# First routed stage of a two-layer macaron transformer: plain indirect writes by first and second choice, added on VectorE, in place of indirect additions to DRAM

## The chip, the cores and the metric

One core of one Trainium2 chip runs the whole network in one program. The metric is the device time of one execution in microseconds, lower is better; the kernel before was timed in three runs. TensorE is the matrix engine (PE in the profile), VectorE is DVE, ScalarE is ACT, GpSimd is POOL and SyncE is SP, which issues most DMAs. The rows "POOLq" and "SPq" are the instruction queues that issue DMAs.

## The reference

Input: x, 8 sequences of 512 tokens of width 128, so 4096 tokens in 32 tiles of 128.

```
x = x + 0.5 * ffn0(layernorm(x))       # 8 experts of 256, top 2, no capacity
x = x + attn0(layernorm(x))            # 32 heads of 32
x = x + 0.5 * ffn0(layernorm(x))
x = x + 0.5 * ffn1(layernorm(x))       # first routed stage
x = x + attn1(layernorm(x))            # 16 heads of 64
x = x + 0.5 * ffn1(layernorm(x))       # second routed stage
```

ffn1 sends each token to its two best experts of eight. Each expert has room for 640 tokens and takes those with the largest weights; what exceeds the room is dropped, so a token may get results from two, one or no expert. An expert computes `(silu(x wg) * (x wu)) wd`, and its row is multiplied by the token's normalised weight and added to the token.

## The kernel before

**Order.** Every engine has an instruction stream of its own, and semaphores tie them. `program_order` gives each part of the work a hand-written start and end on a common scale (the table `WHEN`), sorts the calls, and each engine plays the same list with its own generators, one step per call. So where an engine's instruction stands in its queue is fixed by hand. The parts in order: feedforward 0 (`compute0`, `prepare0`) over 8 sequences and 8 experts; attention 0, 64 groups (8 sequences, 8 groups of heads); feedforward 0 again, with the router of layer 1 beside it (`route`, `keep`); the first routed stage (`experts1(0)`); attention 1, again 64 groups, with `ahead` preparing the next sequence and `route` its router; the second routed stage (`experts1(1)`).

**X** holds the residual of all 4096 tokens on chip. A sequence of 512 tokens is a batch in the code. `x_done[b]` is the event after which VectorE may use sequence b of it.

**The routed stage.** VectorE searches each expert's threshold (`search`), numbers the places (`positions`), and ends with `token_of`: for each of 8 x 5 x 128 slots the number of its token row. It comes from two small matmuls, over the number within a tile and the number of the tile (`tile_number`, written by ScalarE as 1 to 32 for both choices; the choices stand one after the other in it). Empty slots get one of 640 extra rows behind the 4096. Per expert, GpSimd issues five gathers (`gather_rows`, line 1970), each of 128 rows of 544 bytes from the DRAM tensor `tokens`; TensorE turns them (line 785), computes gate and up in three split products each (line 780), and the down projection (line 1115); ScalarE writes the weighted rows to `rows_out` (line 1409), and GpSimd issues five scatters of 128 rows of 512 bytes (`scatter_rows`, line 1982). A scatter is an indirect DMA with `compute_op=ALU.add`. GpSimd's queue is: gathers of experts 0, 1, 2, scatters of 0, gathers of 3, scatters of 1, and so on. Scatters of expert e wait for those of e - 1 to have landed, since two of them may add to the same row.

In the first routed stage the scatters add into the DRAM tensor `sums`. `keep` (SP, line 2084) has stored X there, sequence by sequence, during the second feedforward; at the end SP waits for the last scatter and loads X back with 8 DMAs of 256 KB (line 2003), and attention 1 begins with the layernorm of sequence 0 (line 1441 on VectorE, then GpSimd, then ScalarE, then TensorE's transposes). In the second routed stage the scatters add into the output.

**Attention 1.** For every group, TensorE computes q, k, v (line 780), the scores for the maxima and for the probabilities (line 902), the weighted sums (line 945) and the sums of probabilities (line 984). VectorE takes maxima (line 1583), reciprocals (line 1614), the mixed result (line 1627) and the low halves of q and k (line 1557), which free the banks that the scores of the next group need. GpSimd adds probability tiles (line 1947), two operands on chip. `normalise` (line 1447) is the first step of `ahead` for the next sequence: four statistics and four aggregations, between the reciprocals of a group.

```
def scatter_rows(e):
    pool.wait_ge(sums_stored, 16 * BATCHES * (s + 1))
    if s or e:
        pool.wait_ge(*(all_scattered(s, e - 1) if e else all_scattered(0, EXPERTS - 1)))
```

## Time and profile before

| what | value |
|---|---|
| median of three runs | 3053.96 us (3050.08 to 3054.35) |
| profiled execution | 3044.68 us, span of its trace 3042.9 us |
| busy, share of the span | PE 92%, DVE 69%, ACT 57%, POOL 57% |
| chain that ended last | PE 31%, DVE 4%, POOL 4%, the rest under 10% |
| DMA | 151 MB, mean 50 GB/s |

| stretch, us | what runs | PE busy | DVE busy | POOL busy |
|---|---|---|---|---|
| 0 to 228 | feedforward 0 | 210.65 | 143.83 | 15.55 |
| 228 to 1440 | attention 0 | 1186.84 | 870.50 | 993.02 |
| 1440 to 1640 | feedforward 0, router | 184.35 | 141.67 | 20.51 |
| 1640 to 1699 | first search and places | 16.47 | 45.21 | 0.00 |
| 1699 to 1849 | first routed stage | 107.88 | 53.04 | 106.64 |
| 1849 to 2840 | attention 1 | 960.63 | 756.00 | 509.13 |
| 2840 to 3042 | second search and routed stage | 122.55 | 93.41 | 104.32 |

The profiled execution is the one that every time in the text comes from; it was 9 us shorter than the median of the runs. A busy engine in such a table is not yet the bound: for each stretch one has to ask which wait ends last. In the trace's rows a bracket tells how long the engine was idle before the row and what it waited for; rows that follow each other without one had no wait worth showing.

### The profile page before, as it was taken

Reading aid. Unit: us, or ns where it says so; the run is one execution under the profiler, and the core shown is the slowest. Engines: PE = TensorE matmul, PEld = TensorE weight load, DVE = VectorE, ACT = ScalarE, POOL = GpSimd, SP = SyncE. Lnnn points to the kernel's source line nnn. Section 1 sums busy time; section 2 is a strip of 40 time slices with the busy share of each in tenths; the row PEclk is TensorE's granted clock in tenths of the full one; section 3 lists DMA queues with packets and bytes.
Section 4 is the critical chain, followed back from the end, with each engine's and each line's share of the span. In section 5 each row is a group of like instructions: output and inputs, shape, how many; then the busy total and the mean of one; then the engine's idle time right before and its main releaser. Section 6 shows DMA issues by size and latency. Waiting matters only on the chain. (4 is left out here: it accounts for less than half of the span.)

```text
span 3042.9 us, 49798 instructions
## 1 busy us (share of the span) xinstructions
PE 2789.4 (92%) x17716; PEld 1926.3 (63%) x17716; DVE 2103.6 (69%) x4494; ACT 1735.3 (57%) x3334; POOL 1749.2 (57%) x1540
## 2 busy tenths in 40 slices
PE   7999999999999999999995686999999999999376
PEld 6995555556555565647884584666666666665276
DVE  5667777777776777765776535877878778777642
ACT  5665767676776767676773334554545445445033
POOL 0004989898988888893100473555545555555067
PEclk9999999999999999999997798999999999999588
DMA  3004443343344344330002241000000000000033
GB/s 100 1 7 99 96 92 87 86 104 85 91 92 92 85 92 98 85 78 18 15 23 67 61 69 34 2 5 5 8 5 5 5 9 5 5 5 9 28 80 54
DMA packets 127654, 151.32 MB, mean 50 GB/s; under 512 B 29939, under 2 KB 69424, under 8 KB 126896
## 3 DMA queue, kind: packets, MB, share of 16 engines
q1 hardware_dynamic: 113328, 137.41, 18.5%
q0 software_dynamic: 14080, 10.73, 2.6%
q8 instruction: 143, 2.34, 0.3%
q14 instruction: 103, 0.84, 0.1%
HBM read 31.34 MB, written 14.57 MB: 15 GB/s over the span
## 5 line engine op out<-in xcount | busy, mean ns | idle before, releaser
L1947 POOL TENSOR_TENSOR arena<-arena 128x512 f32<-128x512 f32 x1152 | 1444.5, 1281 | 591.6 <-ACT arena L1304 557.3
L1583 DVE TENSOR_REDUCE top<-psum 128x1 f32<-128x512 f32 x1536 | 973.1, 678 | 193.4 <-PE psum L902 124.4
L1304 ACT ACTIVATE arena<-psum 128x512 f32<-128x512 f32 x1536 | 838.0, 599 | 237.9 <-PE psum L902 141.1
L894 PE MATMUL psum<-stack 96*128 96x512 f32 (+1 forms) x2048 | 648.2, 440 | 16.3 <-ACT arena L1304 9.1
L894 PEld LDWEIGHTS psum<-stack 96*128 96x128 f32 (+1 forms) x2048 | 345.9, 190 | 211.5 <-DVE top L1583 81.5
L945 PE MATMUL psum<-arena,values 128*32 128x512 f32 (+1 forms) x3072 | 476.6, 595 | 3.4 <-ACT arena L1304 3.4
L945 PEld LDWEIGHTS psum<-arena,values 128*32 128x32 f32 (+1 forms) x3072 | 133.3, 119 | 289.7 <-issue 284.5
L902 PE MATMUL psum<-stack 64*128 64x512 f32 x2048 | 293.0, 398 | 12.0 <-DVE top L1583 5.5
L1916 POOL TENSOR_SCALAR rstd<-mv 128x4 f32<-128x4 f32 x56 | 13.0, 233 | 487.2 <-DVE mv L1444 485.3
L1614 DVE RECIPROCAL psum<-psum 128x128 f32<-128x128 f32 x256 | 228.6, 934 | 25.6 <-PE psum L984 25.6
L902 PEld LDWEIGHTS psum<-stack 64*128 64x128 f32 x2048 | 200.9, 184 | 59.1 <-issue 26.3
L902 PE MATMUL psum<-halves 64*128 64x512 f32 x1536 | 231.5, 400 | 0.7 <-issue 0.7
L1318 ACT ACTIVATE arena<-psum 128x512 f32<-128x512 f32 x128 | 76.9, 601 | 259.5 <-PE psum L945 259.5
L780 PE MATMUL psum<-stack 128*128 128x512 f32 x768 | 211.2, 411 | 0.1
L1534 DVE SCALAR_TENSOR_TENSOR X<-psum,weight,X 128x128 f32<-128x128 f32 x512 | 144.0, 344 | 91.4 <-PE psum L846 90.2
L846 PEld LDWEIGHTS psum<-arena 128*128 128x128 f32 x1536 | 184.8, 192 | 7.6 <-issue 1.0
L846 PE MATMUL psum<-arena 128*128 128x128 f32 x1536 | 186.8, 275 | 0.1
L1229 ACT ACTIVATE arena<-arena 128x512 f32<-128x512 f32 x256 | 158.4, 629 | 43.6 <-DVE arena L1525 32.9
L902 PEld LDWEIGHTS psum<-halves 64*128 64x128 f32 x1536 | 149.3, 185 | 33.7 <-issue 12.6
L1970 POOL DMA_INDIRECT arena<-tokens,arena x80 | 83.4, 1043 | 149.2 <-DVE arena L1855 125.4
L1560 DVE TENSOR_TENSOR halves<-psum,halves 128x512 fp32r<-128x512 f32 x128 | 88.4, 691 | 109.4 <-ACT halves L1255 108.2
L780 PEld LDWEIGHTS psum<-stack 128*128 128x128 f32 x768 | 137.2, 192 | 25.1 <-issue 1.3
(182 smaller groups left out, 3787.9 us busy)
## 6 DMA issues: line engine op xcount, KB each, us to landing
stack<-halves SPq DMA_DIRECT2D x768, 128.0 KB, 2.3
tokens<-xn SPq DMA_DIRECT2D x16, 256.0 KB, 2.4
arena<-in_wg SPq DMA_DIRECT2D x16, 256.0 KB, 3.0
arena<-in_wu SPq DMA_DIRECT2D x16, 256.0 KB, 3.4
arena<-in_wd SPq DMA_DIRECT2D x16, 256.0 KB, 2.8
wqkv<-in_w_qkv SPq DMA_DIRECT2D x2, 1536.0 KB, 9.3
X<-in_x SPq DMA_DIRECT2D x8, 256.0 KB, 4.3
sums<-X SPq DMA_DIRECT2D x8, 256.0 KB, 2.8
```

The source lines that it names most:

```text
L780: ins = T_.matmul(out_ap, weights[w], moving[m], start=i == 0, stop=i == 2)
L846: ins = T_.matmul(bk[:, t * P:(t + 1) * P], h[:, c, t * P:(t + 1) * P], w[:, c, :], start=c == 0, stop=c == 1)
L894: return T_.matmul(bk, st[0:k, side, h, cols], st[0:k, 1 - side, h, :], start=True, stop=True)
L902: ins = T_.matmul(bk, weights[rows_h], moving[rows_h], start=r == 0, stop=r == len(rounds) - 1, tile_position=(64 * h, 0))
L945: ins = T_.matmul(bk[c, :], values[:, n % N_VALUES, kt, c], prob[l][(n * TILES_B + kt) % N_PROB[l]][:, h, :], start=kt == 0, stop=kt == TI ...
L1229: S_.activation(part, part, ACT.Square).then_inc(squared, 1)
L1304: S_.activation(prob[l][tile % N_PROB[l]][:, h, :], psum[:, bank[key], :], ACT.Exp, scale=scale).then_inc(released[bank[key]], 1)
L1534: ins = V_.scalar_tensor_tensor(out=X[:, tile, :], in0=psum[:, bank[key], t * P:(t + 1) * P], scalar=weight[:, t, e:e + 1], in1=X[:, tile, ...
L1560: give(V_.tensor_tensor(hv[:, lo, :], psum[:, bank[key], :], hv[:, hi, :].bitcast(fp32), ALU.subtract), key)
L1583: give(V_.reduce_max(top[i][:, column:column + 1], psum[:, bank[key], :], AX.X), key)
L1614: done = tick(V_.reciprocal(psum[:, bank[key], c], psum[:, bank[key], c]))
L1947: ins = G_.tensor_tensor(to[:, h, :], old[:, h, :], prob[l][tile % N_PROB[l]][:, h, :], ALU.add)
```

## The change

The scatters of the first routed stage become plain indirect writes into a new DRAM tensor `made` with two halves: rows 0 to 4095 for the first choice, rows 8192 to 12287 for the second, and the extra rows of empty slots between them. `tile_number` is 1 to 32 for the first choice and 65 to 96 for the second, so VectorE gets the row in `made` (`row_of`) where it got the token; one more operation masks it to the token (`token_of`), in both routed stages. Scatters of the first stage don't wait for each other; two semaphores take turns by expert. `sums`, the eight stores of X into it and the eight loads back are gone. Rows that no expert writes must be zero: 16 loads of a zeroed tile `y` fill `made` at the start (SP), where 5 loads of 64 KB into `sums` were; VectorE zeroes `y` first. At the end of the stage SP loads the two choices for sequences 0 and 1 into two free buffers (in `stack[2]`); the loads for sequence b + 1 are issued in `ahead(1, b)`. In `normalise`, VectorE adds both choices to X, two additions of 128x512, before the statistics.

```diff
+SECOND_CHOICE = P // 2
+        made_rows = [stack[2][:, 1, 2 * i:2 * i + 2, :].bitcast(fp32).rearrange("p k (t d) -> p k t d", d=DIM) for i in range(2)]
-        token_of, empty = carve(SLOT_ROWS), carve(SLOT_ROWS)
+        token_of, row_of, empty = (carve(SLOT_ROWS) for _ in range(3))
-        sums = nc.dram_tensor("sums", ((SLOT_TILES + TILES) * P, DIM), fp32, kind="Internal").ap()
+        made = nc.dram_tensor("made", ((SECOND_CHOICE + TILES) * P, DIM), fp32, kind="Internal").ap()
-        scattered = sem("scattered")
+        scattered = sems("scattered", 2)
+        zeros_set = sem("zeros_set")
+        got_made = sems("got_made", 2)
+        made_added = sem("made_added")
...
         def all_scattered(s, e):
-            return scattered, 16 * SLOT_TILES * (s * EXPERTS + e + 1)
+            slot = e % len(scattered)
+            earlier = sum(m % len(scattered) == slot for m in range(EXPERTS)) if s else 0
+            return scattered[slot], 16 * SLOT_TILES * (earlier + e // len(scattered) + 1)
...
                                           (tile_number.rearrange("p (k t) x -> p k (t x)", k=2),
-                                           count[:, 1:1 + TILES].unsqueeze(1).to_broadcast(each_tile), 1.0)):
+                                           count.rearrange("p (k t) -> p k t", k=TOP_K)[:, :, 1:1 + TILES], 1.0)):
...
             def normalise(key, b):
                 if key[:2] == ("a", 1):
-                    x_done[b] = got_x[b], 32
+                    xb = X[:, b * TILES_B:(b + 1) * TILES_B, :]
+                    dve.wait_ge(got_made[b % 2], 32 * (b // 2 + 1))
+                    for choice in range(TOP_K):
+                        dve.wait_ge(*x_done[b])
+                        x_done[b] = tick(V_.tensor_tensor(xb, xb, made_rows[b % 2][:, choice], ALU.add),
+                                         made_added if choice == TOP_K - 1 else step_done)
...
-                give(V_.scalar_tensor_tensor(
-                    out=bits(token_of), in0=tile_of, scalar=float(P), in1=token_of,
-                    op0=ALU.mult, op1=ALU.add), key)
+                a = tick(V_.scalar_tensor_tensor(
+                    out=bits(row_of), in0=tile_of, scalar=float(P), in1=token_of,
+                    op0=ALU.mult, op1=ALU.add))
+                dve.wait_ge(*a)
+                give(V_.tensor_scalar(bits(token_of), bits(row_of), SECOND_CHOICE * P - 1, None, ALU.bitwise_and), key)
...
+            tick(V_.memset(y[:, :, :], 0.0), zeros_set)
...
                 def scatter_rows(e):
-                    pool.wait_ge(sums_stored, 16 * BATCHES * (s + 1))
-                    if s or e:
-                        pool.wait_ge(*(all_scattered(s, e - 1) if e else all_scattered(0, EXPERTS - 1)))
+                    if s:
+                        pool.wait_ge(sums_stored, 16 * BATCHES)
+                        if e:
+                            pool.wait_ge(*all_scattered(s, e - 1))
...
+                        else:
+                            G_.indirect_dma_start(
+                                made, bass.IndirectOffsetOnAxis(ap=row_of[:, r:r + 1].bitcast(u32), axis=0),
+                                rows_out[e % 2][:, t, :], None, bounds_check=(SECOND_CHOICE + TILES) * P - 1,
+                                oob_is_err=True).then_inc(scattered[e % len(scattered)], 16)
...
-                        load(sums_v[:, TILES + t, :], ident, no_token)
+                    sp.wait_ge(zeros_set, 1)
+                    for choice in range(TOP_K):
+                        for b in range(BATCHES):
+                            first = choice * SECOND_CHOICE + b * TILES_B
+                            load(made_v[:, first:first + TILES_B, :], y[:, :, :], no_token)
...
+            def load_made(b):
+                for choice in range(TOP_K):
+                    first = choice * SECOND_CHOICE + b * TILES_B
+                    load(made_rows[b % 2][:, choice], made_v[:, first:first + TILES_B, :], got_made[b % 2])
+
+            def ahead(l, b):
+                if l and 0 < b < BATCHES - 1:
+                    sp.wait_ge(made_added, b)
+                    load_made(b + 1)
+                yield
...
             def keep(s, b):
                 here = slice(b * TILES_B, (b + 1) * TILES_B)
-                sp.wait_ge(*x_settled(s, b))
-                Y_.dma_start((sums_v, out_v)[s][:, here, :], X[:, here, :]).then_inc(sums_stored, 16)
+                if s:
+                    sp.wait_ge(*read(("out", 1, b)))
+                    Y_.dma_start(out_v[:, here, :], X[:, here, :]).then_inc(sums_stored, 16)
...
-                    sp.wait_ge(*all_scattered(s, EXPERTS - 1))
-                    for b in range(BATCHES):
-                        here = slice(b * TILES_B, (b + 1) * TILES_B)
-                        load(X[:, here, :], sums_v[:, here, :], got_x[b])
+                    for e in range(EXPERTS - len(scattered), EXPERTS):
+                        sp.wait_ge(*all_scattered(s, e))
+                    for b in range(2):
+                        load_made(b)
```

## Rows read from the trace of the kernel before

**Rows 1.** Timeline of GpSimd in the first routed stage: start us, us, engine, line, operation, count.

```profile
1725.68 1.62 POOL L1982 DMA_INDIRECT sums<-arena  x1 [7.02 <-ACT arena L1409]
...
1735.07 1.09 POOL L1970 DMA_INDIRECT arena<-tokens,arena  x1 [0.30 <-issue]
...
1742.20 1.62 POOL L1982 DMA_INDIRECT sums<-arena  x1 [0.30 <-issue]
...
1829.72 1.78 POOL L1982 DMA_INDIRECT sums<-arena  x1 [2.37 <-DMA sums<-arena]
```

**Rows 2.** Timeline of TensorE in the same stage.

```profile
1718.88 0.71 PE L785 MATMUL psum<-cst,arena 128*128 128x128 f32 x5
1719.71 4.73 PE L1115 MATMUL psum<-arena 128*128 128x128 f32 x40
1724.20 7.30 PE L780 MATMUL psum<-halves,stack 128*128 128x320 f32 x48
1731.34 0.71 PE L785 MATMUL psum<-cst,arena 128*128 128x128 f32 x5
...
1744.13 0.77 PE L785 MATMUL psum<-cst,arena 128*128 128x128 f32 x5 [0.17 <-DMA arena<-tokens,arena]
...
1808.06 0.77 PE L785 MATMUL psum<-cst,arena 128*128 128x128 f32 x5 [3.67 <-DMA arena<-tokens,arena]
...
1814.68 7.29 PE L780 MATMUL psum<-halves,stack 128*128 128x320 f32 x48
1822.64 4.73 PE L1115 MATMUL psum<-arena 128*128 128x128 f32 x40 [0.67 <-DVE arena L1892]
```

**Rows 3.** Scatters and gathers by line: count, duration ns min/median/max, first and last start.

```profile
L1982 POOL DMA_INDIRECT sums<-arena x40: 1552/1554/1783, 1725.7 to 1837.4; - x40
...
L1970 POOL DMA_INDIRECT arena<-tokens,arena x80: 992/998/1555, 1699.0 to 3005.4; - x80
```

**Rows 4.** Chain that ended last, at the end of the stage: start us, us, what.

```profile
1837.39 3.27 DMA sums<-arena
```

**Rows 5.** Table by stretch: length, busy us and count per engine, clock, DMA share, GB/s.

```profile
40.00:60.00 20.00, 20.00 (x143) 18.29 (x142) 12.86 (x43) 13.39 (x25) 1.70 (x4) 1.00 0.00 1
2240.00:2360.00 120.00, 118.24 (x784) 78.05 (x783) 94.70 (x162) 59.99 (x115) 63.93 (x56) 1.00 0.02 6
```

**Rows 6.** VectorE timeline: the last step of token_of, start us, us.

```profile
1697.88 0.20 DVE L1855 SCALAR_TENSOR_TENSOR arena<-psum,arena 128x40 int32<-128x40 f32 x1
```

**Rows 7.** The first two reloads of X on SP's queue, by tile.

```profile
L2003 SPq DMA_DIRECT2D X<-sums x2: 378/443/508, 1840.7 to 1841.1; - x2
...
DMA to landing us min/median/max: 2.9/3.1/3.3
```

**Rows 8.** VectorE additions with two on-chip inputs, by line; GpSimd idle, then adding.

```profile
L1481 DVE TENSOR_TENSOR stack<-arena,stack x4: 684/685/693, 20.6 to 22.5; 128x512 fp32r<-128x512 f32 x4
L1481 DVE TENSOR_TENSOR stack<-wqkv,stack x4: 677/1738/1757, 1377.0 to 1382.0; 128x512 fp32r<-128x512 f32 x4
```

**Rows 9.** VectorE timeline at the start of the program.

```profile
4.50 0.87 DVE L1441 BATCH_NORM_STATS2 stats<-X 128x6 f32<-128x128 f32 x4 [3.34 <-DMA X<-in_x]
```

**Rows 10.** Timelines of GpSimd and VectorE, short windows near 1377 and 2041.

```profile
1376.93 1.27 POOL L1947 TENSOR_TENSOR arena<-arena 128x512 f32<-128x512 f32 x1
1377.03 1.73 DVE L1481 TENSOR_TENSOR stack<-wqkv,stack 128x512 fp32r<-128x512 f32 x1 [5.88 <-ACT stack L1174]
...
2040.69 1.28 POOL L1947 TENSOR_TENSOR arena<-arena 128x512 f32<-128x512 f32 x1
```

**Rows 11.** Timeline of VectorE in attention 1, at the statistics for sequence 2.

```profile
2040.35 0.81 DVE L1441 BATCH_NORM_STATS2 stats<-X 128x6 f32<-128x128 f32 x4
...
2044.79 0.74 DVE L1557 SCALAR_TENSOR_TENSOR stack<-psum,bqk,stack 128x512 fp32r<-128x512 f32 x1
```

**Rows 12.** Timeline of TensorE in attention 1, after the statistics of sequences 1 and 2.

```profile
1926.72 0.96 PE L902 MATMUL psum<-stack 64*128 64x512 f32 x6 [0.72 <-DVE stack L1557]
...
2049.69 0.98 PE L902 MATMUL psum<-stack 64*128 64x512 f32 x6 [0.42 <-ACT arena L1304]
```

More of the change, by code:

```diff
@@ L599, in build @@
         tokens = nc.dram_tensor("tokens", ((SLOT_TILES + TILES) * P, DIM + EXPERTS), fp32, kind="Internal").ap()
-        sums = nc.dram_tensor("sums", ((SLOT_TILES + TILES) * P, DIM), fp32, kind="Internal").ap()
+        made = nc.dram_tensor("made", ((SECOND_CHOICE + TILES) * P, DIM), fp32, kind="Internal").ap()
         tokens_v = tokens.rearrange("(t p) d -> p t d", p=P)
-        sums_v = sums.rearrange("(t p) d -> p t d", p=P)
+        made_v = made.rearrange("(t p) d -> p t d", p=P)
         out_rows = out.rearrange("b s d -> (b s) d")
@@ L651, in build @@
         no_token, weights_stored, sums_stored = sem("no_token"), sem("weights_stored"), sem("sums_stored")
-        scattered = sem("scattered")
+        scattered = sems("scattered", 2)
+        zeros_set = sem("zeros_set")
+        got_made = sems("got_made", 2)
+        made_added = sem("made_added")
         N_SMALL, TABLES = 9, 9
+        ROWS_WITHOUT = 16 * (2 * SLOT_TILES + TOP_K * BATCHES)
         def written(key):
@@ L701, in all_scattered @@
         def all_scattered(s, e):
-            return scattered, 16 * SLOT_TILES * (s * EXPERTS + e + 1)
-        def x_settled(s, b):
-            return read(("out", 1, b)) if s else read(("down", 1, b, EXPERTS - 1))
+            slot = e % len(scattered)
+            earlier = sum(m % len(scattered) == slot for m in range(EXPERTS)) if s else 0
+            return scattered[slot], 16 * SLOT_TILES * (earlier + e // len(scattered) + 1)
         def experts_in(sems_, s, e, each):
@@ L1367, in make_tables @@
                     act.wait_ge(constants_set, 1)
-                    each_tile = [P, 2, TILES]
                     for to, of, scale in ((same_bf16, same_expert, 1.0), (share_bf16, share, 1.0),
@@ L1648, in project_out @@
                         dve.wait_ge(y_normed, b)
+                    else:
+                        dve.wait_ge(no_token, ROWS_WITHOUT)
                     dve.wait_ge(*written(key))
@@ L1962, in gather_rows @@
                         pool.wait_ge(*event)
-                    pool.wait_ge(no_token, 48 * SLOT_TILES)
+                    pool.wait_ge(no_token, ROWS_WITHOUT)
                     pool.wait_ge(weights_stored, 16 * BATCHES * (s + 1))
@@ L1981, in scatter_rows @@
                         pool.wait_ge(*read(("narrow", s, e, t // 4)))
-                        G_.indirect_dma_start(
-                            (sums, out_rows)[s], bass.IndirectOffsetOnAxis(ap=token_of[:, r:r + 1].bitcast(u32), axis=0),
-                            rows_out[e % 2][:, t, :], None, bounds_check=(TILES if s else SLOT_TILES + TILES) * P - 1,
-                            oob_is_err=s == 0, compute_op=ALU.add).then_inc(scattered, 16)
+                        if s:
+                            G_.indirect_dma_start(
+                                out_rows, bass.IndirectOffsetOnAxis(ap=token_of[:, r:r + 1].bitcast(u32), axis=0),
+                                rows_out[e % 2][:, t, :], None, bounds_check=TILES * P - 1, oob_is_err=False,
+                                compute_op=ALU.add).then_inc(scattered[e % len(scattered)], 16)
+                        else:
+                            G_.indirect_dma_start(
+                                made, bass.IndirectOffsetOnAxis(ap=row_of[:, r:r + 1].bitcast(u32), axis=0),
+                                rows_out[e % 2][:, t, :], None, bounds_check=(SECOND_CHOICE + TILES) * P - 1,
+                                oob_is_err=True).then_inc(scattered[e % len(scattered)], 16)
                 gather_rows(0)
@@ L2082, in keep @@
                 here = slice(b * TILES_B, (b + 1) * TILES_B)
-                sp.wait_ge(*x_settled(s, b))
-                Y_.dma_start((sums_v, out_v)[s][:, here, :], X[:, here, :]).then_inc(sums_stored, 16)
+                if s:
+                    sp.wait_ge(*read(("out", 1, b)))
+                    Y_.dma_start(out_v[:, here, :], X[:, here, :]).then_inc(sums_stored, 16)
                 sp.wait_ge(routed, s * BATCHES + b + 1)
@@ L2130, in _ @@
             play(order, dict(load0=load0, load_attention=load_attention, project=project, rows=rows_of_maxima,
-                             route=route, keep=keep, experts1=experts1))
-            sp.wait_ge(*all_scattered(1, EXPERTS - 1))
+                             ahead=ahead, route=route, keep=keep, experts1=experts1))
+            for e in range(EXPERTS - len(scattered), EXPERTS):
+                sp.wait_ge(*all_scattered(1, e))
             for event in all_tokens_sent(1):
```

## The prediction

> **What bounds the kernel now.** The place of the change was read first, as the timelines of GpSimd and TensorE in the first routed stage, then the stage that receives its result, attention of layer 1, by the table by stretch and the VectorE timeline.
>
> In the routed stage two queues compete. TensorE alone needs 12.46 us per expert: from the transposes of expert 1 at 1718.88 to those of expert 2 at 1731.34 [rows 2]. GpSimd issues five scatters (1725.68 to 1735.07, 9.39 us) and five gathers (to 1742.20, 7.13 us) per expert, 16.52 us in all [rows 1], so from expert 3 on TensorE waits for gathered rows: expert 7 is transposed at 1808.06 and not at 1718.88 + 6 x 12.46 = 1793.64. An accumulating scatter occupies GpSimd for 1554 ns, a gather for 998 ns [rows 3]. After the last product the chain is serial: last scatter issued at 1837.39, landed 3.27 us later [rows 4], X reloaded, normalised.
>
> In attention of layer 1 TensorE is the bound: busy 118.24 of 120 us at full clock, VectorE 94.70 [rows 5]. The mean slack of VectorE says little. What matters is its queue where the change puts the additions.
>
> **The stage, part by part.** *Scatter price.* No plain indirect write is in the trace. Bounds: the accumulating scatter, 1554 ns, and the gather, 998 ns, also a plain copy of 128 rows with an index each [rows 3]. Nothing excludes less than that, but below it TensorE bounds and little is left to win. I take 998 ns, the nearest in what is computed.
>
> *Pace.* A scatter block becomes 9.39 - 5 x (1.554 - 0.998) = 6.61 us. With gather blocks of 7.13 GpSimd's pace is 13.74 us. The gathers of expert 3 start at 1725.68 + 6.61 = 1732.29; before, they started at 1735.07 and the transposes followed at 1744.13, 9.05 us later [rows 1, 2]. Expert 7, four paces on, is transposed at 1732.29 + 54.96 + 9.05 = 1796.3. With gather blocks as short as five times 1.30 us (0.998 and the 0.30 us between them) it would be 1732.29 + 4 x 13.11 + 8.4 = 1793.1, and TensorE's own pace, 1793.64, holds. I take the middle, 1795.0, and 0.24 us for the added VectorE operation that makes row_of and token_of two steps: these tiny dependent operations cost 0.20 and a gap [rows 6]. So 1795.2, a gain of 12.9 us.
>
> The gather block is longer than 6.5 us because some gathers last up to 1555 ns [rows 3], which I ascribe to VectorE operations with two on-chip inputs running beside them. The Trainium skill, SBUF — State Buffer, "Who interferes with whom", says such an operation takes only the read interface of the shared pair, where generating descriptors needs the write interface, so that nothing should collide; by that the stage would gain about 1.3 us more than my middle.
>
> *To the last product.* Expert 1 went from transposes to gate products in 5.32 us (1724.20), expert 7's gate products to the last down projection in 7.96 (1814.68 to 1822.64): 13.28 us, where the slower clock made it 14.58 [rows 2]. Fewer waits should keep the clock up: 1.3 us more, 14.2 us at the last product.
>
> *Tail.* Expert 0's scatter started 5.97 us after its down projection (1719.71, 1725.68), expert 7's 7.08 us after (1822.64, 1829.72), since it waited for expert 6's landing [rows 1, 2]. That wait goes: 1.1 us. From first to last of the five 7.67 us becomes about 5.3: 2.4 us. I leave the landing at 3.27 us [rows 4]. The stage gains 14.2 + 3.5 = 17.7 us before its costs.
>
> *Costs on the path.* Batch 0 needs two reads of made where one of X was enough: the second was issued at 1841.1, 0.4 us after the first, and the slower landing was 3.3 us against 2.9 [rows 7]: 0.9 us. Then two dependent additions of 128x512 at 0.685 us [rows 8] with their gaps: 1.43 us, GpSimd idle there. The second routed stage has the added VectorE operation too: 0.24 us. Net of the stage: 17.7 - 2.6 = 15.1 us gained.
>
> **Costed at nothing.** The eight stores of X into sums leave SP's queue in feedforward 2; their cover is that TensorE bounds there. The zeros: 16 loads of 256 KB follow the weights on SP. SP has no further work until attention 0, and the DMA engines are idle at 40 to 60 us [rows 5]; without that cover their issues alone, 16 of 0.44 us [rows 7], would cost 7 us. Clearing y on VectorE falls into its 3.34 us of waiting for X [rows 9]. Two reads per batch on SP in attention come where SP only feeds maxima rows for the next group. The waits on made_added and got_made look back a whole batch of 121 us.
>
> **What attention 1 pays.** The two additions for batches 1 to 7 stand in VectorE's queue just ahead of the statistics of that batch, between reciprocals. For batch 2 that is 2040.35; from there VectorE runs without a pause up to the second k/q subtraction (2044.79, 0.74 us), which releases TensorE's scores [rows 11]. GpSimd at that moment still adds probabilities: its last one runs from 2040.69 for 1.28 us [rows 10]. All six batches 2 to 7 show these times in the same phase.
>
> What an addition with two on-chip inputs costs beside GpSimd is shown by the weight split: 685 ns with GpSimd idle, 1738 ns median with GpSimd adding [rows 8]. In detail, the one issued at 1377.03 ended at 1378.76, 0.56 us after GpSimd's operation had ended at 1378.20 [rows 10]: they take turns, and a turn of GpSimd is then 1.738 - 0.56, about 1.15 us. Applied to 2040.35: the first addition waits until GpSimd's fifth ends at 2040.69 and itself ends at 2041.25; GpSimd's sixth then runs until 2042.40; the second addition until 2042.96. So 2.6 us where an idle GpSimd would give 1.43. The ends of the range are 1.43 and 2 x 1.74 = 3.5 us.
>
> Does TensorE feel it? In batch 1 it already waited 0.72 us for VectorE's subtraction: all 2.6 us are lost. In batches 2 to 7 it did not wait there, and I give it no slack, since the subtraction ended just as it got to the scores; but a later wait of 0.42 us for ScalarE goes [rows 12]. 6 x (2.6 - 0.42) + 2.6 = 15.7 us. TensorE cannot catch up, being the bound. GpSimd's own 0.4 us of delay has a group to spend.
>
> **Sum.** -15.1 + 15.7 = +0.6 us. The profiled execution took 3044.7 us, its span 3042.9; the median of the three runs is 3054.0, 9.3 us above it. I make the sum against the former and carry it over: 3045.3 for a profiled one, 3054.6 for the median. The measurement can tell about 0.2%, 6.1 us.
>
> **The rivals.**
> *Additions at the idle price.* The turns with GpSimd don't happen or the phase shifts: 6 x (1.43 - 0.42) + 1.43 = 7.5 us; -15.1 + 7.5 = -7.6, 3046.4. For it: GpSimd has only 1.6 us left when the additions start. Against: the weight split rows.
> *TensorE feels nothing.* VectorE's slack of 25 us in 120 [rows 5] absorbs them: -15.1, 3038.9. Against: TensorE's 0.72 us wait in batch 1 [rows 12].
> *The plain write costs the issue as much as the accumulating one* (slower). Place: GpSimd's queue in the routed stage. Its pace stays 16.5 us and only the wait of 1.1 us goes: -1.1 + 2.6 + 15.7 = +17.2, 3071.2. Each 0.1 us of a scatter above 0.998 costs about 2 us over four paces plus 0.4 in the tail; it turns measurably slower from some 1.23 us. For it: the index handling is the same. Against: the gather handles indices too, at 998 ns. The Trainium skill, DMA: Bandwidth & Descriptors, "SWDGE vs HWDGE vs iDMA", has GpSimd write one pair of descriptors per plain transfer, read and write; by it the plain write costs like the gather. No run here shows it yet.
> *The additions cost their full 3.5 us*, GpSimd winning both turns: 6 x 3.08 + 3.5 = 22.0; +6.9, 3060.9.
>
> **Chances.** The forecast 0.47; idle price 0.22; nothing felt 0.08; plain write dear 0.13; full contention 0.10. Within its own error of 4 us the forecast is the same in 0.40, faster 0.03, slower 0.04; idle price is faster in 0.17, same in 0.05; nothing felt faster; dear write slower; full contention half and half. Faster 0.28, same 0.50, slower 0.22. Range 3041 to 3066: it takes in the idle price and full contention with the clock's 1 or 2 us, and leaves out most of the two cases at its ends; the forecast's own is 3050 to 3060.
>
> **What would show it.** Plain scatters of about 1.0 us; TensorE at 12.5 to 13 us per expert; last scatter near 1820, reads of made issued near 1823 where those of X were at 1840.7. In attention 1 the first addition near 0.9 and the second near 1.7 us, a new TensorE wait for VectorE's subtraction of some 2.6 us once per batch, and a batch period some 2.2 us longer. Wrong if the scatter keeps 1.5 us, or the waits per batch are under 1 us.

## The result, and the profile after

The change took 3086.15 us in the median (3082.50 to 3087.69, four runs), the kernel before 3052.42 (3050.08 to 3054.35, a fourth run added to the three of the forecast): a ratio of 1.0107, 95% interval 1.0095 to 1.0119, 34 us slower. The forecast was 3054.6 within 3041 to 3066, so it was wrong. The profiled execution took 3082.5 us, its span is 3080.3.

The span cut at the starts of the first gather and the last scatter of each routed stage and of the first and last group of statistics of attention 1 (us; "stage" below is the column stage 1; the row "again" is the same changed kernel, experiment e9 below):

| kernel | to first gather | stage 1 | to statistics | attention 1 | search | stage 2 | rest | span |
|---|---|---|---|---|---|---|---|---|
| before | 1699.0 | 138.4 | 6.2 | 988.8 | 66.0 | 138.8 | 5.7 | 3042.9 |
| after | 1703.0 | 146.6 | 7.5 | 1007.2 | 66.4 | 142.6 | 7.0 | 3080.3 |
| again | 1702.4 | 119.8 | 7.6 | 1004.5 | 66.4 | 138.2 | 6.9 | 3045.8 |

Of the 37.4 us between the first two rows 18.4 are in attention 1, where 15.7 were forecast, and 8.2 in the stage that was to gain 17.7 up to its last scatter. The rest is spread over parts whose code hardly changed. The 4.0 us ahead of the first gather are no effect of the change: over all profiles here that gather starts between 1698.6 and 1703.9 us, with either kernel's code.

**GpSimd in the changed stage**, timeline of after: start us, us, engine, line. It answers to [rows 1].

```profile
1756.34 1.05 POOL L1985 DMA_INDIRECT arena<-tokens,arena  x1 [0.30 <-issue]
...
1761.62 1.00 POOL L1985 DMA_INDIRECT arena<-tokens,arena  x1 [0.31 <-issue]
1766.22 1.04 POOL L2004 DMA_INDIRECT made<-arena  x1 [3.60 <-ACT arena L1414]
1767.56 1.16 POOL L2004 DMA_INDIRECT made<-arena  x1 [0.30 <-issue]
1769.03 0.98 POOL L2004 DMA_INDIRECT made<-arena  x1 [0.30 <-issue]
...
1771.60 0.98 POOL L2004 DMA_INDIRECT made<-arena  x1 [0.30 <-issue]
1772.89 1.05 POOL L1985 DMA_INDIRECT arena<-tokens,arena  x1 [0.30 <-issue]
...
1782.67 1.04 POOL L2004 DMA_INDIRECT made<-arena  x1 [3.51 <-ACT arena L1414]
```

The plain scatter costs 0.98 us, as forecast. Block of scatters 6.67 us (1766.22 to 1772.89), where it was 9.39. But ahead of each block GpSimd now waits 3.5 us for ScalarE's rows, and the pace is 1782.67 - 1766.22 = 16.45 us per expert, the old 16.5. Who holds ScalarE? The timelines of TensorE and ScalarE for the same expert, number 2 (its scatters are those from 1766.22 on):

```profile
1755.36 0.71 PE L791 MATMUL psum<-cst,arena 128*128 128x128 f32 x5
1756.79 4.96 PE L1121 MATMUL psum<-arena 128*128 128x128 f32 x40 [0.72 <-issue]
```

```profile
1758.31 0.77 ACT L1356 ACTIVATE halves<-psum 128x512 fp32r<-128x512 f32 x2 [2.37 <-remote]
1764.27 1.40 ACT L1414 ACTIVATE arena<-psum,arena 128x128 f32<-128x128 f32 x5 [5.19 <-remote]
```

ScalarE may evict the first four tiles once 32 of TensorE's 40 products of L1121 are done, at about 1756.79 + 0.8 x 4.96 = 1760.8. It starts at 1764.27, idle for 5.19 us until "remote": the profile found no instruction on this core that ended then. The event of the semaphore that ScalarE waits for stands some 3.5 us behind the end of those products, and ScalarE starts 1.65 us after the issue of GpSimd's last gather (1761.62 + 1.00). Below this is called a late signal. The same steps for expert 4 in the profile of the row "again", the repeat, GpSimd, TensorE and ScalarE:

```profile
1775.32 1.05 POOL L1985 DMA_INDIRECT arena<-tokens,arena  x1 [0.30 <-issue]
...
1780.61 0.99 POOL L1985 DMA_INDIRECT arena<-tokens,arena  x1 [0.30 <-ACT arena L1401]
1781.90 1.04 POOL L2004 DMA_INDIRECT made<-arena  x1 [0.30 <-issue]
```

```profile
1773.13 4.73 PE L1121 MATMUL psum<-arena 128*128 128x128 f32 x40
```

```profile
1777.09 1.40 ACT L1414 ACTIVATE arena<-psum,arena 128x128 f32<-128x128 f32 x5 [3.39 <-PE psum L1121]
```

Here the products allow it at 1773.13 + 0.8 x 4.73 = 1776.9 and ScalarE starts at 1777.09, in the middle of the gathers; the scatters follow with only the usual gap. To count late signals, each TensorE instruction that signals is set against the next event of its semaphore, and those are taken that come 0.1 to 8 us after its end. Some signals of the slow traces have no event of their own, so the counts are rough. In the first stage of the after profile 22 of 25 signals given during a block of gathers were late, 37 of 82 during a block of scatters and 10 of 37 at other times; in the trace of before and in the repeat not one was.

**Attention 1**, VectorE and TensorE at the additions of sequence 2, from the repeat; they answer to [rows 11, 12]:

```profile
2029.78 2.61 DVE L1458 TENSOR_TENSOR X<-X,stack 128x512 f32<-128x512 f32 x2
2032.43 0.87 DVE L1446 BATCH_NORM_STATS2 stats<-X 128x6 f32<-128x128 f32 x4
```

```profile
2037.82 1.11 PE L908 MATMUL psum<-stack 64*128 64x512 f32 x6 [2.50 <-DVE stack L1567]
```

and TensorE's waits in attention 1 in the after profile (the repeat has the same first row):

```profile
PE psum L908 <- DVE stack L1567: 18.2, 7, 3.1
```

Two additions take 2.61 us, seven waits make 18.2 us, and the period of a sequence goes from 121.0 us to 123.1 in the repeat.

### The profile page after: what moved, and what is told of

Same layout as the page of the kernel before. It is cut to its first block and busy times, and to the rows that moved or that the text cites. A ratio compares the mean times of both kernels' runs of the same rounds, so it can differ in the third digit from the quotient of the medians.

```text
span 3080.3 us, 49822 instructions
## 1 busy us (share of the span) xinstructions
PE 2805.4 (91%) x17716; PEld 1929.0 (63%) x17716; DVE 2124.3 (69%) x4513; ACT 1736.5 (56%) x3334; POOL 1730.6 (56%) x1540
## 3 DMA queue, kind: packets, MB, share of 16 engines
q1 hardware_dynamic: 121056, 141.27, 18.6%
## 5 line engine op out<-in xcount | busy, mean ns | idle before, releaser
L908 PE MATMUL psum<-stack 64*128 64x512 f32 x2048 | 295.0, 401 | 27.0 <-DVE stack L1567 18.2
L1544 DVE SCALAR_TENSOR_TENSOR X<-psum,weight,X 128x128 f32<-128x128 f32 x512 | 144.1, 344 | 91.3 <-PE psum L852 90.1
L908 PEld LDWEIGHTS psum<-halves 64*128 64x128 f32 x1536 | 149.0, 186 | 35.5 <-issue 12.6
```

What stands on the lines that cost most here:

```text
L908: ins = T_.matmul(bk, weights[rows_h], moving[rows_h], start=r == 0, stop=r == len(rounds) - 1, tile_position=(64 * h, 0))
L1544: ins = V_.scalar_tensor_tensor(out=X[:, tile, :], in0=psum[:, bank[key], t * P:(t + 1) * P], scalar=weight[:, t, e:e + 1], in1=X[:, tile, ...
```

## The experiments

The experiments ran in six sets, here called occasions. Each gave traces without a late signal or with many, never mixed within an occasion:

| runs | kernel before, us | late signals in the profiles |
|---|---|---|
| e1 to e4 | 3057.22 | 91 to 116 in each |
| e5 to e8 | 3047.19 | none |
| e9, e10 | 3049.12 | none |
| e11 to e13 | 3048.35 | none |
| e14 to e16 | 3056.25 | 98 to 144 |
| e17, e18 | 3054.12 | 99, 102 |

**e1, e2, e3: is it a place in memory?** The change puts row_of between token_of and empty and makes the DRAM tensor larger. e1 puts row_of behind the other tiles; e2 and e3 give the kernel before the new places.

```diff
# e1, on the change
-        token_of, row_of, empty = (carve(SLOT_ROWS) for _ in range(3))
+        token_of, empty = carve(SLOT_ROWS), carve(SLOT_ROWS)
...
+        row_of = carve(SLOT_ROWS)
...
# e2, on before
-        token_of, empty = carve(SLOT_ROWS), carve(SLOT_ROWS)
+        token_of, _, empty = (carve(SLOT_ROWS) for _ in range(3))
# e3, on before
-        sums = nc.dram_tensor("sums", ((SLOT_TILES + TILES) * P, DIM), fp32, kind="Internal").ap()
+        sums = nc.dram_tensor("sums", ((P // 2 + TILES) * P, DIM), fp32, kind="Internal").ap()
```

> The change as it is, with the 40 words of row_of placed behind all other tiles of the routed stage, so that empty, rows_in, gated and rows_out stand where the kernel before had them. Theory L (layout): the 160 bytes by which the change moves these tiles are what delays the semaphores in both routed stages; then the stages lose their disturbance, first stage some 20 us shorter than in the change and second some 5 us, so about 3060 us. Rival N (not layout): 3086 us as the change, with late semaphores as before.

Measured: 3088.37 us, ratio 1.0102 (1.0083 to 1.0122); stage 148.0.

> The kernel before with 40 unused words in front of empty, so that the same tiles stand where the change has them. Theory L: both routed stages get late semaphores, each 5 to 10 us longer, 3062 to 3072 us. Rival N: 3052 us.

Measured: 3058.99 us, ratio 1.0003 (0.9993 to 1.0013).

> The kernel before with the DRAM tensor sums as large as made (6.3 MB instead of 2.4). Theory M (place in DRAM): what lies behind in DRAM moves and both routed stages are disturbed, 3062 to 3072 us. Theories L and others: 3052 us.

Measured: 3057.52 us, ratio 1.0005 (0.9996 to 1.0015). None of the places tried matters. But both profiles of what is in effect the kernel before showed late signals too, with stages of 143.8 and 144.3 us where its own profile had 138.4. So the lateness is not the change's (theories L and M fall); the kernel before pays 5.4 and 5.9 us for it in the stage and 3.8 and 5.7 in the second. In the stage it pays once, ahead of its very first scatter, where GpSimd waits for ScalarE's rows 12.6 us in e2 (7.02 in [rows 1]); from there on it keeps its pace of 16.5 us or less. GpSimd's wait for ScalarE in e2's first stage:

```profile
POOL sums L1982 <- ACT arena L1409: 12.6, 1, 12.6
```

**e4: additions for sequence 0 alone** (leaves out the experts' results of sequences 1 to 7).

```diff
-                    for choice in range(TOP_K):
+                    for choice in range(TOP_K if b == 0 else 0):
...
-                    sp.wait_ge(made_added, b)
+                    sp.wait_ge(made_added, 1)
```

> The change without the additions for batches 1 to 7 (the results of the experts are left out for them); loads as in the change. If these additions cost in attention 1 what the forecast gave them, about 16 us go: 3070 us. If the 18.5 us that attention 1 lost are a disturbance like that of the routed stages, 3080 us or more.

Measured: 3065.04, 1.0024 (1.0014 to 1.0034); attention 1 989.1 us against 1010.3 in e1 beside it. The additions of sequences 1 to 7 are worth 21 us there, more than the 16 expected, and even without them the change is not faster: its stage took 150.5.

**e5: scatters that accumulate** in the changed kernel, so that each costs 1.55 us again.

```diff
-                                oob_is_err=True).then_inc(scattered[e % len(scattered)], 16)
+                                oob_is_err=True, compute_op=ALU.add).then_inc(scattered[e % len(scattered)], 16)
```

> The change with its scatters of the first routed stage made accumulating again (they add onto the zeros of made; same result), nothing else. A scatter goes back from 983 to about 1554 ns. Theory G: the stage is not paced by the price of a scatter, but by a loop in which TensorE's signals arrive late while gathers are being issued, the scatters of an expert wait for such a signal, and the gathers wait for those scatters; then dearer scatters cost little or nothing, first stage 144 to 150 us from first gather to last scatter (the change 146.6 to 150.5), total within 3 us of the change. Rival P (price paces): five scatters per expert, 2.8 us dearer, make the stage 15 us longer, 3100 us.

Measured: 3068.13, 1.0067 (1.0050 to 1.0084); stage 138.4. Read against the result this looked as if dear scatters cost nothing; but the occasion had no late signals, and e9 shows that the change itself takes 119.8 there. e12 repeats it beside the change.

**e6: the additions moved.** Those of sequences 1 to 7 leave the place ahead of the statistics and stand behind maxima rows of two earlier groups, five and four before the end of the sequence ahead.

```diff
+            if l == 1 and b and g == 0:
+                for back in (5, 4):
+                    when = at + n - back + 1.821
+                    stream("gain", (b,), 1, 1, when, when)
...
-                if key[:2] == ("a", 1):
...
# the body of that branch is now the generator gain(b), one addition a step
+                if key == ("a", 1, 0):
+                    for _ in gain(0):
+                        pass
```

> The change with the additions for batches 1 to 7 moved in VectorE's queue: one each behind the low half of the maxima rows of the groups five and four before the batch, where VectorE and GpSimd both had nothing to do in the trace of before. If they cost by their place, attention 1 goes from 1007 to 1010 us back to about 990, total near 3066 us. If VectorE's 14 x 0.7 us cost anywhere, 10 us of it stay.

Measured: 3028.33, 0.9941 (0.9925 to 0.9958): it beats both. VectorE's additions in attention 1 and TensorE's waits for VectorE there, from the profiles of the moved version (e18 for the first row, e6 for the second):

```profile
L1461 DVE TENSOR_TENSOR X<-X,stack 128x512 f32<-128x512 f32 x14 | 9.4, 671 | 0.0
```

```profile
PE psum L912 <- DVE stack L1576: 0.4, 1, 0.4
```

671 ns each instead of 1.3 us, and 0.4 us of waits where there were 18.2. Attention 1 takes 987.4 us, less than the 988.8 of before.

**e7, e8: gathers and scatters one by one in turn**, in e6's kernel and in before; three experts gathered ahead, then one scatter, one gather. `steps` takes one DMA from each of the given parts in turn.

```diff
...
-                for e in range(EXPERTS):
-                    if e + 2 < EXPERTS:
-                        gather_rows(e + 2)
-                    scatter_rows(e)
+                for e in range(3):
+                    steps(gather_rows(e))
+                for e in range(EXPERTS):
+                    steps(scatter_rows(e), *([gather_rows(e + 3)] if e + 3 < EXPERTS else []))
```

> As e6, and in both routed stages GpSimd issues scatters of expert e and gathers of expert e + 3 in turn, one by one, instead of five and five. Theory G: with no block of five gathers the signals get through sooner and the loop of 16.6 us per expert falls to the 13 us that ten issues of 1.3 us need, first stage near 125 us, total near 3045 us. Rival: signals are late whatever the order, the stage stays at 146 us or more, total 3066 us.

> The kernel before with the same interleaving of scatters and gathers in both routed stages. Its GpSimd queue was full already (9.4 and 6.6 us per expert), so nothing to win beyond late signals at the start: both theories 3052 to 3060 us; over 3 us shorter would say that late signals cost the kernel before too.

Measured: 3038.43, 0.9966 (0.9954 to 0.9977), and 3057.23, 1.0034 (1.0021 to 1.0046). Both are 10 us worse than with blocks (e6 and before), mostly in the stages whose scatters accumulate: the second takes 144.1 in e7, where e6 has 138.2, and 144.5 in e8, whose first takes 143.9. The plain stage of e7 takes 121.5 where e6 has 119.8. The accumulating scatters of an expert wait for the landing of those of the expert before, and a block of gathers in between covered that landing. In turns nothing does; GpSimd's waits for it in the first stage of before and of e8:

```profile
POOL sums L1982 <- DMA sums<-arena: 4.8, 2, 2.5
```

```profile
POOL sums L1986 <- DMA sums<-arena: 11.3, 7, 2.4
```

The 6.5 us more account for the 5.5 us by which the stage grew. On late signals these two runs say nothing, since their occasion had none.

**e9, e10: the change itself again**, nothing edited, beside the moved version.

> The changed kernel itself, nothing edited, beside the kernel before and beside the version with its additions moved. In the profile of the change its first routed stage (first gather to start of last scatter) took 146.6 us with signals of TensorE that reached ScalarE up to 7 us late; the version with moved additions, whose code in that stage is the same, took 119.8 us and none of its signals was late. Theory C (the lateness belongs to the chip or to the execution, not to the program): where the profiles of this call show no late signals, this kernel's first routed stage takes about 120 us, at 12.5 us per expert, and its time is the kernel before +0 to +6 us (the stage gives 18, the additions and the clock take 18 to 24); where they do show them, the stage takes 144 to 150 us and the time is the kernel before +26 to +36 us, and the version with moved additions is slower than the kernel before -19 as well. Theory K (the lateness belongs to the changed program): the stage is 144 to 150 us and the time +26 to +36 us here although the profiles of the version with moved additions in the same call show no late signals.

Measured: 3051.13 us (3047.92 to 3056.20, 11 runs), 1.0010 (1.0001 to 1.0019): 2.0 us over the kernel before, whose profile and stages are in the table above. Theory C (the lateness is not the program's) stands, K (it is) falls. GpSimd's waits, 1742 to 1842 us, in this profile and in the after profile:

```profile
POOL made L2004 <- ACT arena L1414: 9.0, 2, 6.3
```

```profile
POOL made L2004 <- ACT arena L1414: 23.8, 6, 6.0
```

> The change with the additions of batches 1 to 7 moved, once more, on the chip on which the changed kernel itself runs in this call. Its attention 1 should again take 987 to 989 us (the change 1007 to 1012). Theory C: if the profiles of this call show late signals of TensorE, its first routed stage takes 144 to 150 us instead of 119.8 and its time is the kernel before +5 to +12 us; if they show none, 120 us and -17 to -21 us. Theory K: 120 us and -17 to -21 us, whatever the changed kernel shows beside it.

Measured: 3031.26 us, ratio 0.9939 (0.9925 to 0.9953), stage 119.8.

**e11, e12, e13: change, accumulating change, moved version** on one occasion.

> The changed kernel itself once more, as the marker of the chip that this call gets. Two profiles of it so far: first routed stage 146.6 us with late signals of TensorE, and 119.8 us with none. Theory C (lateness belongs to the chip, each chip keeping to its kind): with late signals 144 to 150 us in the stage and the kernel before +26 to +36 us; without, 119 to 121 us and +0 to +6 us. Rival (lateness comes and goes between executions on one chip): the times of this kernel's runs lie in two groups some 25 to 35 us apart.

Measured: 3050.14, 1.0009 (0.9999 to 1.0019), one group of ten runs (3045.88 to 3060.19), stage 119.4. Attention 1 took 1010.6, 6 us more than in e9, with six short stretches of TensorE at half its clock ("dips", see the part on attention 1 below) where e9 had two. This set carries the chip number of e1 to e4, which had late signals, so the part of theory C by which each chip keeps to its kind is not borne out.

> The change with scatters that accumulate in the plain rows, so that each costs GpSimd about 1.55 us instead of 0.98. On a chip without late signals: first routed stage 138.4 us and attention 1 as in the change, so the changed kernel +15 to +20 us. On a chip with them, theory G (the pace is then set by a loop through a late signal of TensorE that falls into the issue of the gathers, in which shorter scatters only add waiting): stage 141 to 150 us, within 5 us of the changed kernel's or below it, time within 6 us of it or less. Theory P (there GpSimd's own work still sets the pace, each scatter at its price): the changed kernel +14 to +19 us there too.

Measured: 3070.73, 1.0077 (1.0060 to 1.0094), stage 135.9. So on such an occasion the cheaper scatter is worth 20.6 us (16.5 in the stage), and of e12's theories G (a loop through a late signal sets the pace, so the scatter's price counts little) and P (GpSimd's own work sets it, late signals or not) neither was tested. GpSimd's scatters, after 1715 us, in e12 and then in e9:

```profile
L2004 POOL DMA_INDIRECT made<-arena x40 | 63.5, 1587 | 20.4 <-issue 11.3 <-ACT arena L1414 8.8 <-ACT arena L1401 0.3
```

```profile
L2004 POOL DMA_INDIRECT made<-arena x40 | 40.8, 1019 | 27.4 <-ACT arena L1414 16.2 <-issue 11.0 <-ACT arena L1401 0.3
```

> The change with the additions of batches 1 to 7 moved behind the maxima of the batch ahead. On a chip without late signals: the kernel before -17 to -21 us, as twice before. On a chip with them: stage 144 to 150 us, attention 1 at 987 to 990 us, so the changed kernel -18 to -24 us and the kernel before +4 to +12 us (no version of plain rows is then faster than before).

Measured: 3031.64, 0.9942 (0.9925 to 0.9958).

**e14, e15, e16: the lateness made by hand.** e14 holds ScalarE's evictions of experts 0 to 5 until the gathers two experts ahead have landed; e15 (change) and e16 (before) put three copies of 128x512 ahead of them.

```diff
# e14
                         act.wait_ge(*written(key))
+                        if s == 0 and part == 0 and e + 2 < EXPERTS:
+                            act.wait_ge(rows_ready[i], 16 * SLOT_TILES * ((e + 2) // 2 + 1))
# e15, e16
                         act.wait_ge(*written(key))
+                        for k in (range(3) if s == 0 and part == 0 else ()):
+                            S_.activation(spare[k], psum[:, bank[key], :], ACT.Copy)
```

> The changed kernel, in which ScalarE holds its five evictions of an expert's result (experts 0 to 5 of the first routed stage) until the gathers of the expert two ahead have landed: the lateness of TensorE's signal made by hand, on whatever chip. Theory G (on chips with late signals the pace is the loop gathers, late signal, evictions, scatters): six experts go from 13.1 us of GpSimd's own pace to about 6.6 for the gathers, 2 for their landing, 2.0 for the evictions and 6.45 for the scatters, 17 us; the stage from 119.8 to 140 to 148 us, against 146.6 in the profile of the change, and the time +20 to +28 us on the change. Rival (GpSimd keeps enough work waiting to cover a held signal): stage below 128 us, time within 8 us of the change.

> The changed kernel with 1.8 us of idle work for ScalarE (three copies of 128x512 to a buffer that nobody reads) between TensorE's signal and the evictions of each expert's result in the first routed stage: every signal of that kind late by a fixed 1.8 us. If any such lateness were enough, the stage grows by 8 x 1.8 = 14 us or more (134 or above). If only lateness until the end of the gathers counts (theory G) and GpSimd is the bound at 13.1 us per expert with its next rows already evicted, the stage stays within 119 to 124 us and the time within 5 us of the change's.

> The kernel before with the same 1.8 us of idle ScalarE work before the evictions of each expert. GpSimd is busy 16 us per expert there and the rows are evicted earlier still against its scatters: stage 138 to 141 us, the time within 3 us of the kernel before. If fixed lateness counted in the change (14 us or more in the run beside) but not here, it would be the reason why only the change suffers on chips with late signals.

Measured, on an occasion with late signals: e14 3087.82, 1.0103 (1.0086 to 1.0120), stage 147.8; e15 3097.63, 1.0132 (1.0115 to 1.0149), stage 161.6; e16 3056.88, 1.0003 (0.9993 to 1.0012), stage 144.4. A hold until the gathers land adds nothing to the 146.6 to 150.5 us that this stage took with late signals anyway (after, e1, e4): the evictions already wait that long. In the kernel before a gather lands 2.6 us after its start in the median, 1.6 us after its issue of 1.0, and the evictions in after start 1.65 us after the last gather's issue, so the late signal comes at about that landing; whether the landing is what releases it no run shows. A fixed 1.8 us added 11 to 15 us to these, where 8 x 1.8 is 14.4: the loop that sets the pace runs through this signal and this eviction. In before it added nothing (144.4 against 143.8 and 144.3 in e2 and e3). The numbers expected for e14 and e15 on an occasion without late signals were not put to the test. GpSimd's waits in the stage in e14, e15, e16, and in e3:

```profile
POOL made L2006 <- ACT arena L1416: 25.0, 6, 6.0
```

```profile
POOL made L2007 <- ACT arena L1417: 33.2, 6, 7.5
```

```profile
POOL sums L1985 <- issue: 9.7, 32, 0.3
POOL arena L1973 <- issue: 7.0, 23, 0.3
POOL sums L1985 <- DMA sums<-arena: 4.9, 2, 2.5
```

```profile
POOL sums L1982 <- issue: 9.4, 31, 0.3
POOL arena L1970 <- issue: 7.6, 25, 0.3
POOL sums L1982 <- DMA sums<-arena: 4.9, 2, 2.5
```

In before no wait of GpSimd for ScalarE over 0.3 us appears in this window: its dearer scatters leave the rows ready when it comes to them.

**e17, e18: the hold again, and the moved version again.**

> The changed kernel with ScalarE's evictions of experts 0 to 5 held until the gathers of the expert two ahead have landed, on another occasion. With late signals of TensorE it took 147.8 us in the first routed stage, as the change itself (146.6), so the hold added nothing there. On an occasion without them, theory G says that the hold alone makes the slow stage: 140 to 148 us instead of 119.8, the time +20 to +28 us on the kernel before. Rival (something else of those occasions lengthens the stage): below 130 us. On one with them: 146 to 149 us again.

> The change with the additions of batches 1 to 7 moved, once more. Without late signals: stage 119 to 120 us, the kernel before -17 to -21 us. With them: stage 146 to 149 us, attention 1 at 987 to 990 us, the kernel before +4 to +12 us, so that this version then beats the change but not the kernel before.

Measured, with late signals again: e17 3082.50, 1.0096 (1.0079 to 1.0112), stage 146.9; e18 3061.26, 1.0027 (1.0017 to 1.0036), stage 147.4, attention 1 988.3. ScalarE's wait in e17 now has a name, the landing of the gathers, and a length of 5.6 us each, where "remote" had 5.3 us each in the change (26.7 us in 5 waits in after):

```profile
ACT arena L1416 <- DMA arena<-tokens,arena: 27.8, 5, 6.7
```

## Why the prediction was wrong

**The steps of the stage were right, where no signal is late.** Forecast: expert 7's transposes 1795.2 - 1699.0 = 96.2 us after the first gather. The repeat, TensorE's timeline, with the first gather at 1702.4:

```profile
1797.21 0.71 PE L791 MATMUL psum<-cst,arena 128*128 128x128 f32 x5
1798.05 4.73 PE L1121 MATMUL psum<-arena 128*128 128x128 f32 x40
1802.54 7.29 PE L786 MATMUL psum<-halves,stack 128*128 128x320 f32 x48
1810.50 4.73 PE L1121 MATMUL psum<-arena 128*128 128x128 f32 x40 [0.68 <-DVE arena L1906]
```

94.8 us, TensorE's own pace of some 12.46 per expert: the lower of the two ends between which I took the middle. The block of gathers lasted 6.58 us (1775.32 to 1781.90), where [rows 1] had 7.13. The Trainium skill, SBUF — State Buffer, "Who interferes with whom", by which a VectorE operation with two on-chip inputs should not hold up the making of descriptors, had also put the stage 1.3 us under the middle. The traces don't bear out its reason, and the measurement decides: the four gathers of the repeat that lasted 1.31 to 1.49 us, and the five of before with 1.42 to 1.56, each started with 0.27 to 0.62 us of such an operation still to run, while gathers that met one at another point took 0.99 to 1.12. In the repeat's first stage only the very first gather met one in this way. To the start of the last scatter the stage gained 18.6 us, forecast 17.7. And the plain write costs like the gather, 0.98 against 1.00 us. That agrees with the Trainium skill, DMA: Bandwidth & Descriptors, "SWDGE vs HWDGE vs iDMA", by which each plain transfer is one pair of descriptors, read and write. *Costs*: from the last scatter to the statistics 1.4 us more, where 0.9 and 1.43 were taken. Behind the last scatter of the second stage the repeat takes 1.2 us more than before, which no term of the sum had.

**Attention 1: the mechanism was right, its price too low in most traces.** Forecast 15.7 us, measured 15.7 in the repeat; two additions 2.6 us forecast and 2.61 measured; a TensorE wait of 2.6 forecast and 2.50 measured. What was not in the sum is the clock: behind some of these waits TensorE has 3.4 us at half speed. Table by stretch of the after profile (us, busy us and count of PE, PEld, DVE, ACT, POOL, clock, DMA share, GB/s), the second stretch being the one right behind the first:

```profile
1942.60:1946.00 3.40, 3.40 (x20) 3.09 (x18) 1.29 (x2) 1.09 (x2) 0.00 (x0) 0.50 0.03 7
1946.00:1949.40 3.40, 3.40 (x31) 2.70 (x27) 2.58 (x4) 1.65 (x4) 3.23 (x3) 1.00 0.00 0
```

20 products against 31. A dip of 3.4 us at half the clock costs at most 1.7 us (an estimate). Attention 1 had two in e9 (1004.5 us), three in after (1007.2), six in e11 (1010.6) and six, two of them of double length, in e5 (1012.4), and none of this kind in before, in e4 or in the moved version. (A longer one near its end is in every kernel.) Over the nine traces with the additions in this place they cost 15.2 to 23.6 us, six of them over 20. That the repeat met the forecast to the tenth is luck: it is one of the two with the fewest dips.

**Sum where no signal is late**: +0.6 forecast, +2.0 and +1.8 measured between medians. The repeat's span is 2.9 us over that of before: -18.6 in the stage, +1.4 behind it, +15.7 in attention 1, +1.2 at the end, -0.2 in the second search and stage, and +3.4 ahead of the first gather, within the spread of that start given above.

**The step that failed** is the one that put the sum on the measured kernel: "I make the sum against the former and carry it over". With it went its largest term, "The stage gains 14.2 + 3.5 = 17.7 us": in the measured kernel the stage lost 8.2 us. The profiled execution of before was 9.3 us faster than the median, and I took the gap for an offset that both kernels share. Part of it may be the mark of late signals, which that trace did not show: the kernel before takes 3047 to 3049 us in the median on occasions without them and 3054 to 3057 with them, and its four runs here (3052.42) lie in between. Whether they had late signals no trace shows; the after profile had 104. What such an execution costs depends on the kernel. In the kernel before, GpSimd's 16.5 us per expert cover a late signal from the second expert on (e2, e3, e16). The change takes 2.7 us off GpSimd's block, so that TensorE's signal for the rows of expert e falls into the gathers of e + 2; where it comes only after they end, the evictions, the scatters and the next gathers follow in series: 1.65 + 1.95 to the first scatter, 6.67 of scatters, 6.28 of gathers, 16.5 us. The gain goes to a new wait. Between the two profiles of the same kernel that is 146.6 - 119.8 = 26.8 us of stage: 3.3 up to the first scatter, 16.7 in the five paces from there to expert 5's (16.5 us each against 13.2), 6.8 behind that. With 4.4 in the second stage and 2.7 in attention 1, of which its one dip more makes at most 1.7, it comes to 33.9 of the 34.5 us between the two spans.

**The rivals.** None held. The dear plain write gave +17 by the right place, GpSimd's queue, and the wrong cause: the scatter costs 0.98 us. The full price of the additions, 22.0 us, is near what most traces show in attention 1, but by the clock and not by GpSimd winning both turns: two additions took 2.61 us and not 3.5. No rival had a wait for ScalarE in place of the time removed, though [rows 1] show one of 7.02 us ahead of the very first scatter.

**What stays open.** What makes the signals late, and what decides the kind of occasion: not the program, nor anything an edit here touched; the first and the fourth set of runs even carried the same chip number, one with and one without. That the hold alone makes the slow stage was not seen on an occasion without late signals. Between G and P no accumulating version ran beside late signals; e15 and e16 speak for G, since 1.8 us on ScalarE lengthened the stage of the change and not that of before.

## What to carry to other kernels

Shortening one of two parts that cover each other gains only as long as the signals in between are prompt: ask what the new loop goes through, and price it with a late signal. Where a profile is a third of a per cent off the median of its own runs, find out what differs before taking its slack as given, and repeat a change on another occasion before judging it: here the same program was 2 us or 34 us slower. And put VectorE's work with two inputs on chip where neither GpSimd's adding nor TensorE's next operand is near: seven pairs of additions cost 15 to 24 us in one place and nothing measurable a few groups earlier, which alone makes the change faster than before (0.994), though with late signals still 1.0027.

## What the hardware showed unexpectedly

Signals of TensorE can reach ScalarE and VectorE up to 7 us late in both routed stages (91 to 144 of them in an execution), or not one in an execution of the same program. In the after profile most of those given while GpSimd issued gathers were late (22 of 25), fewer of those during scatters (37 of 82), and behind each of the last five blocks of gathers there the first signal came 1.45 to 1.54 us after the block's end. After waits of TensorE for VectorE of some 2.5 us inside otherwise dense work, two to six of seven were followed by a stretch of 3.4 us, in three cases 6.8, at half the clock.
